# Routed attention of a four-layer kernel: the exponentials scaled by their sums on VectorE ahead of the transposes, the reciprocals' spreading matmuls removed, the attention output copied by ScalarE

## The reference, cut to what matters

```python
def _L0_ffn_ref(x, Wq, bq, Wk, bk, Wv, bv, Wr, br, Wo, bo):
    N_HEAD = 16; N_ACTIVE = 4; D_ATTN = 64
    dist = jax.nn.softmax(jnp.mean(x @ Wr + br, axis=1), axis=-1)
    _, idx = jax.lax.top_k(dist, N_ACTIVE)
    idx = jnp.sort(idx, axis=-1)
    ...
    Qs, Ks, Vs = (gather(Q), gather(K), gather(V))
    scale = 1.0 / jnp.sqrt(jnp.asarray(D_ATTN, x.dtype))
    score = jax.nn.softmax(jnp.einsum('bhqd,bhkd->bhqk', Qs, Ks) * scale, axis=-1)
    O = jnp.einsum('bhqk,bhkd->bhqd', score, Vs)
    O = O.transpose(0, 2, 1, 3).reshape(b, s, N_ACTIVE * D_ATTN)
    return O @ Wo + bo
```

## Time and profile before

| | us |
|---|---|
| time before, median of 3 runs | 599.1 (597.71 to 599.11) |
| the profiled execution, its own time | 606.65 |
| its span in the trace | 604.8 |
| PE busy | 511.8 (85%) |
| DVE busy | 381.9 (63%) |
| ACT busy | 272.9 (45%) |

### The profile page before, as it was taken

One profiled execution on the slowest core, in us unless ns is written; L12 is line 12 of the kernel. 1 busy time (PEld: TensorE's weight loads), 2 busy tenths in 40 slices (PEclk: granted clock), 3 DMA queues, 4 the chain that ended last, 5 costly groups with the idle time before them and its releaser, 6 DMA issues.

```text
span 604.8 us, 9328 instructions
## 1 busy us (share of the span) xinstructions
PE 511.8 (85%) x3141; PEld 354.3 (59%) x3141; DVE 381.9 (63%) x1362; ACT 272.9 (45%) x842; POOL 152.5 (25%) x179
## 2 busy tenths in 40 slices
PE   3921899978879899989878978979999999689976
PEld 2300788956744467675546445765666666358845
DVE  4899958462684576844659446755444444699766
ACT  2778557331223566613344425623222222489453
POOL 4999943040247000002102531110000000300032
PEclk9755599989798999997886977987999999899989
DMA  7003000000281000000010030000000000000001
GB/s 271 28 10 130 2 2 1 2 1 28 112 348 51 1 2 1 2 2 1 0 32 21 22 94 1 2 1 1 1 1 1 1 0 2 0 1 1 3 0 36
DMA packets 8197, 18.37 MB, mean 30 GB/s; under 512 B 1043, under 2 KB 6227, under 8 KB 7638
## 3 DMA queue, kind: packets, MB, share of 16 engines
q1 hardware_dynamic: 8150, 17.78, 8.2%
HBM read 15.99 MB, written 1.79 MB: 29 GB/s over the span
## 4 chain that ended last, share of the span: by engine, by line
PE 66%; POOL 13%; DVE 11%; ACT 5%; issue 3%; DMA 1%; SPq 0%; DVEq 0%; POOLq 0%; ACTq 0%
PE bank L1775 6%; PE bank L1776 6%; PE bank L1786 6%; PE bank L248 3%; PE bank L1022 3%; PE bank L1961 3%; PE bank L762 3%; PE bank L1066 3%; PE bank L1045 2%; POOL rstd L206 2%; PE bank L1937 2%; PE bank L728 2%; ACT arenaB L1977 2%; PE bank L241 2%; PE bank L843 2%
## 5 line engine op out<-in xcount | busy, mean ns | idle before, releaser
L205 POOL TENSOR_SCALAR rtmp<-mv 128x4 f32<-128x4 f32 x22 | 5.1, 231 | 329.3 <-DVE mv L191 329.2
L1827 DVE TENSOR_TENSOR arenaB<-arenaB,bank 128x512 f32<-128x512 f32 x40 | 27.5, 687 | 54.9 <-PE bank L1776 54.0
L1797 ACT ACTIVATE arenaB<-bank 128x512 f32<-128x512 f32 x40 | 24.0, 599 | 76.9 <-PE bank L1775 76.8
L1786 PEld LDWEIGHTS bank<-arenaA,arenaB 128*128 128x128 f32 x320 | 38.7, 192 | 9.1 <-issue 9.1
L248 PE MATMUL bank<-in_ctx 128*128 128x512 f32 (+1 forms) x114 | 43.4, 528 | 0.0
L1775 PE MATMUL bank<-xnT,arenaA 128*128 128x512 f32 x80 | 42.8, 618 | 0.0
L1776 PE MATMUL bank<-xnT,arenaA 128*128 128x512 f32 x80 | 42.0, 606 | 0.0
L1786 PE MATMUL bank<-arenaA,arenaB 128*128 128x128 f32 x320 | 38.8, 275 | 0.0
L248 PEld LDWEIGHTS bank<-in_ctx 128*128 128x128 f32 x114 | 20.3, 210 | 17.7 <-issue 17.5
L1977 ACT ACTIVATE arenaB<-bank,arenaB 128x77 f32<-128x77 f32 x88 | 27.2, 347 | 5.9 <-DVE arenaB L2000 5.9
L1776 PEld LDWEIGHTS bank<-xnT,arenaA 128*128 128x128 f32 x80 | 15.8, 197 | 20.2 <-issue 20.2
(11 more groups left out here) (472 smaller groups left out, 1283.3 us busy)
## 6 DMA issues: line engine op xcount, KB each, us to landing
arenaA<-in_moe_dram SPq DMA_DIRECT2D x1, 3840.0 KB, 11.5
in_dft<-in_dft_dram SPq DMA_DIRECT2D x1, 2048.0 KB, 7.5
in_dft<-in_head_dram SPq DMA_DIRECT2D x1, 2048.0 KB, 7.6
arenaA<-in_l_dram SPq DMA_DIRECT2D x1, 2048.0 KB, 16.0
vw_scratch<-in_dft SPq DMA_DIRECT2D x32, 38.5 KB
arenaB<-vw_scratch SPq DMA_DIRECT2D x2, 576.0 KB, 4.8
in_rows<-in_rows_dram SPq DMA_DIRECT2D x1, 842.5 KB, 7.2
in_ctx<-in_ctx_dram SPq DMA_DIRECT2D x1, 653.0 KB, 6.5
```

Source lines behind the costliest of these rows:

```text
L1786: ins = nc.tensor.matmul(bank[4 + m % 3][:, q4 * P:(q4 + 1) * P], hid2[:, m % 2, c, q4 * P:(q4 + 1) * P], w[:, 2 * HE + c * P:2 * HE + (c ...
L1797: nc.scalar.activation(sil2[:, n % 3, :], bank[n % 2][:], ACT.Silu).then_inc(silu_ready, 1)
L1827: Vv.tensor_tensor(hid2[:, m % 2, c, :], sil2[:, n % 3, :], bank[2 + n % 2][:], ALU.mult).then_inc(hid_ready, 1)
```

## The change

The division moves. DVE, right behind the reciprocals of unit n-1, multiplies each head's exponentials (128x512, in place in `pb0`) by their reciprocal, a pointer scalar. PE's turn of unit n-1 no longer waits for the exponentials but for these products, head by head (`p_norm`). The spreading matmuls, the copy of their result on ACT and DVE's multiplication of the output go. The output is copied from its bank to `oT0` by ACT, behind the exponentials of the pass. The other hunks only take the 16 counts of the stage off the semaphore `rb_copy` and `rb_mm` that a later stage shares.

```diff
@@ pe_attend0
                 m = n - 2
                 if 0 <= m < NU:
                     t, pair = m // 2, m % 2
-                    own, other = bank[6 + m % 2], bank[6 + (m + 1) % 2]
-                    pe.wait_ge(rinv_ready, m + 1)
-                    if m:
-                        pe.wait_ge(o_norm, m)
-                    for i in range(2):
-                        h = 2 * pair + i
-                        ins = nc.tensor.matmul(other[DF * i:DF * (i + 1), AT_R], rinv0[:, t, h:h + 1].broadcast_to([P, DF]), ident,
-                                               start=True, stop=True)
-                    ins.then_inc(rb_mm, 1)
+                    own = bank[6 + m % 2]
                     pe.wait_ge(pT_dve, m + 1)
                     pe.wait_ge(pT_act, m + 1)
-                    if m:
-                        pe.wait_ge(rb_copy, m)
+                    if m >= 2:
+                        pe.wait_ge(o_copy, m - 1)
...
                 m = n - 1
                 if 0 <= m < NU:
-                    pe.wait_ge(sc_exp, 2 * (m + 1))
...
                     for i in range(2):
+                        pe.wait_ge(p_norm, 2 * m + i + 1)
                         for k in range(TB):
@@ vec_attend0
                     Vv.reciprocal(rinv0[:, t, hs], rsum0[:, t, hs]).then_inc(rinv_ready, 1)
+                    dve.wait_ge(rinv_ready, m + 1)
+                    for i in range(2):
+                        h = 2 * (m % 2) + i
+                        Vv.tensor_scalar(pb0[:, m % 2, i, :], pb0[:, m % 2, i, :], rinv0[:, t, h:h + 1], None, ALU.mult).then_inc(p_norm, 1)
                 m = n - 2
-                if 0 <= m < NU:
-                    dve.wait_ge(rb_copy, m + 1)
-                    dve.wait_ge(pv_mm, m + 1)
-                    if m >= 4:
-                        dve.wait_ge(wo_mm, m // 2 - 1)
-                    Vv.tensor_tensor(oT0[:, m % 4, :], bank[6 + m % 2][:, AT_O], rb0[:, m % 2, :], ALU.mult).then_inc(o_norm, 1)
@@ act_attend0
             for n in range(NU + 2):
-                m = n - 2
-                if 0 <= m < NU:
-                    act.wait_ge(rb_mm, m + 1)
-                    if m >= 2:
-                        act.wait_ge(o_norm, m - 1)
-                    nc.scalar.copy(rb0[:, m % 2, :], bank[6 + (m + 1) % 2][:, AT_R]).then_inc(rb_copy, 1)
                 if n < NU:
...
+                m = n - 2
+                if 0 <= m < NU:
+                    act.wait_ge(pv_mm, m + 1)
+                    if m >= 4:
+                        act.wait_ge(wo_mm, m // 2 - 1)
+                    nc.scalar.copy(oT0[:, m % 4, :], bank[6 + m % 2][:, AT_O]).then_inc(o_copy, 1)
                 m = n - 1
                 if 0 <= m < NU:
                     act.wait_ge(sc_turned, 2 * m + 2)
```

More of the change, by code:

```diff
@@ L883, in program @@
         pT0 = part(arenaB, 10240, 2, 2, S)
-        rb0 = part(arenaB, 13056, 2, P)
         oT0 = part(arenaB, 13312, 4, P)
@@ L900, in program @@
         sc_mm, sc_max, sc_exp, sc_turned = sem("sc_mm"), sem("sc_max"), sem("sc_exp"), sem("sc_turned")
-        pT_dve, pT_act, pv_mm, o_norm, wo_mm, x_added = (
-            sem("pT_dve"), sem("pT_act"), sem("pv_mm"), sem("o_norm"), sem("wo_mm"), sem("x_added"))
+        pT_dve, pT_act, pv_mm, o_copy, p_norm, wo_mm, x_added = (
+            sem("pT_dve"), sem("pT_act"), sem("pv_mm"), sem("o_copy"), sem("p_norm"), sem("wo_mm"), sem("x_added"))
         rinv_ready, rb_mm, rb_copy = sem("rinv_ready"), sem("rb_mm"), sem("rb_copy")
@@ L1049, in pe_attend0 @@
                     t = m // 2 - 1
-                    pe.wait_ge(o_norm, m)
-                    pe.wait_ge(rb_copy, min(m + 1, NU))
+                    pe.wait_ge(o_copy, m)
                     for c in range(2):
@@ L1641, in pe_attend2 @@
                     if t:
-                        pe.wait_ge(rb_copy, NU + t)
+                        pe.wait_ge(rb_copy, t)
                     for k in range(TB + 1):
@@ L1653, in pe_attend2 @@
                     pe.wait_ge(oT2_ready, t + 1)
-                    pe.wait_ge(rb_copy, NU + min(t + 2, NT))
+                    pe.wait_ge(rb_copy, min(t + 2, NT))
                     nc.tensor.matmul(bank[6 + t % 2][:, AT_W], oT2[:, t % 2, :], V["wo2T"], start=True, stop=True).then_inc(wo2_mm, 1)
@@ L1696, in vec_attend2 @@
                 if 0 <= t < NT:
-                    dve.wait_ge(rb_copy, NU + t + 1)
+                    dve.wait_ge(rb_copy, t + 1)
                     dve.wait_ge(pv2_mm, t + 1)
@@ L1721, in act_attend2 @@
                 if 0 <= t < NT:
-                    act.wait_ge(rb_mm, NU + t + 1)
+                    act.wait_ge(rb_mm, t + 1)
                     if t >= 2:
```

## The result

The changed kernel takes 614.3 us (median of 4 runs, 612.94 to 617.19) against 599.1. The ratios of this text come from the fast runs of both kernels (a fourth run of the kernel before, at 609.23, was a slow one) and not from the two medians, whose quotient would be 1.0254; this one is 1.0214, 95% interval 1.0149 to 1.0278. The changed kernel took nearly the same time in both; the kernel before was faster in its few first runs. By the two ratios the change makes the kernel slower by 10 to 13 us; 9.9 were forecast. Both intervals are clear of no change; only the second point estimate lies under 2%, and neither interval excludes 2%.

The account below looks back on a forecast made before the run. PE was taken to bound the stage, then a loop through DVE. Terms +0.9, +7.5, +0.7 and +0.8 gave +9.9 us on 606.65, 1.63%, so 599.1 x 1.0163 = 608.9 us; range about 604.5 to 615.

Parts of the forecast that it names:

- the loop: In each pass: scores, both maxima, reciprocals, one scaling, turn, next scores; pass 4.13 us long; chance 80%.
- The signs: Changed profile: PE about 75%, turn released by DVE's scaling, about 480 ns; equal 4.13 us passes; DVE idle before maxima; clock 1.00.
- three signs of being wrong: Maxima sooner than 1.16 us after the scores, scaling under 0.3 or over 0.6 us, or clock below 1.00 before 263 us.
- The removal: Spreading matmuls taken from PE: 0.27 us a pass, a gain only if PE stays full, which was not expected.
- start: First turn of the stage, held until the first scaling is done: +0.9 us.
- middle: Units 2 to 15: 13 passes of 4.13 us, 53.7 against 46.20, +7.5 us.
- the layer norm: Inside passes 11 and 12, its DVE work delays the maxima by 0.4 and 0.3 us: +0.7 us.
- The end: Value products of unit 14 wait for ACT's copy, 4.90 instead of 4.09 us after the last scores: +0.8 us.
- The clock: Rival: PE's rests drop the granted clock to 0.50, about 30 us more, about 639 us in full; chance 5%.
- The copy on ACT: New output copy behind the exponentials is off the path; without that cover, less than 0.3 us a pass.
- The rival that ends faster: PE stays the bound because scaled exponentials are ready in time; about 596 us; chance 3%.
- The rival of one element a cycle: DVE's scaling takes 0.69 us, the pass becomes 4.44 us; about 613.5 us; chance 8%.

Follow-up runs that it names:

- e2: Changed kernel with the scaled exponentials written to an unread tile and the turn waiting for the unscaled exponentials again; ratio to the kernel before 0.9985, stage 59.14 us.
- e5: Changed kernel with one more scaling of the same size, into an unread tile, between reciprocals and first scaling; one profile, stage 77.00 us, passes 4.58 and 4.59.
- e6: Changed kernel with reciprocals and both scalings of unit n-1 moved ahead of the maxima of unit n on DVE; ratio to the kernel before 0.9982, stage 61.82 us.
- e7: Changed kernel with reciprocals and both scalings moved between the first and second maximum of a pass on DVE; one profile, stage 65.26 us.
- e3: Changed kernel without scalings or their wait, spreading still removed, DVE multiplying the output by a constant tile; ratio to the kernel before 0.9916, stage 57.72 us.
- e1: The changed kernel run again, unedited, beside the kernel before; ratio 1.0167 (1.0122 to 1.0211), medians 613.4 against 604.4 us, stage 72.67 us.
- e11: The changed kernel profiled a third time, unedited, for the clock alone; own time 608.94 us, stage 72.29 us.
- e4: Changed kernel with filler matmuls in PE's waits ahead of the turns and the last two value products; ratio to the kernel before 1.0186, stage 70.44 us.

## Why the prediction was right

**The bound and the loop.** Right in mechanism and near in size. The turn is released at 3.19 instead of 3.11 and the pass is 4.19 instead of 4.13. The scaling was well priced; the difference is the time from its end (225.90 + 0.48 = 226.38) to PE's weight load (226.50), 0.12 where 0.07 was taken from ACT's copy, and another 0.03 from the load to the first transpose, which the sum left out. e2 shows that the wait alone makes the loop, e5 that what stands in it counts one to one, e6 and e7 that DVE's order decides where the scaling stands in it.

**The signs.** Of those that the prediction named, the equal passes, the releaser, the 480 ns and DVE's idle time ahead of the maxima came out. PE was to be busy for about 75% and was for 83% (34.73 of 42 us): the 3.05 of 4.13 that it took for a pass leaves out the projection, which stands in every second one, as its own 2.6 says. And one of its three signs of being wrong appeared: the clock fell below 1.00 in the stage.

**The removal.** 0.27 in a pass was forecast if PE stayed full; e3 measured 0.22, the distance in passes rather than between starts.

**Term by term**, e1 against before: start 5.38 - 4.41 = +1.0 (0.9 forecast); middle 54.83 - 46.21 = +8.6 (7.5 and 0.7 for the layer norm, 8.2). In it the layer norm's passes are 4.46 and 4.32, 0.4 over 4.19 together and not 0.7: in the first profile of the change the maxima start 1.47 (249.95 - 248.48) and 1.30 (254.24 - 252.94) into these passes instead of 1.17, so they are late by 0.30 and 0.13, where 0.4 and 0.3 were worked out. The end: 10.84 - 10.06 = +0.8 where the clock holds (e11), as forecast. Together 10.4 against 9.9.

**The clock**, given 5% as a rival in full, came in a small part: about 1.2 us at the start (5.13 - 4.19 and 5.66 - 5.38) and 1.6 at the end (12.46 - 10.84), each in some executions. That is the step of the prediction that was too confident. It argued from 200 to 208 that a PE busy for 71% keeps its clock, and for the passes this held: 1.00 in the middle of e1. What it did not look at are the single rests ahead of and behind them. Before, PE waited 1.40 ahead of the first turn; the change made it 2.40, as a row above shows, and the sum had priced only the 0.9 of delay.

**The copy on ACT** cost nothing in the passes, as forecast: it follows the last accumulator read, and ACT then idles for 0.75 until the turn is done. The rival that ends faster did not happen; e3 shows what it would have been worth. The rival of one element a cycle is excluded by the 484 ns, and so is the 0.33 us that the prediction kept apart from its sum.

**The whole.** 10.4 us and up to 2.8 for the clock are 1.7 to 2.2% of the profiled 606.65; the two comparisons gave 1.67 and 2.14%, where 1.63 was forecast. Since the change is in the stage and the scatter is outside it, I take the difference between the two for scatter and these falls, which no run here separates.

**Where luck had a part.** The forecast in us, 608.9, hangs on the 599.1 of three runs. The measured 614.3 is 5.4 above it and only 0.7 below the upper end of the range, which was set at 615 for a slow scaling that did not come. Of the 5.4, 2.4 come from that base: 599.1 x 1.0214 is 611.9. The sound test is the ratio, and both intervals hold the 1.0163. The prediction also took 0.3% for the least difference that can be told; the intervals here reach 0.3 to 0.65% to either side.

## What to carry to other kernels

An engine at 100% tells what removing its work is worth, not what a new wait costs it: lay one pass out with its start as zero, mark when the operand of the new wait can be ready, and compare with the moment at which the waiting engine gets there. Here 0.22 us a pass was removed and the turn moved back by 0.88, since the new work stood behind two maxima in VectorE's order that had to wait for scores themselves. Before giving up such a change, try the same instructions at another place: ahead of the maxima, or with a buffer and a pass between maker and user, the same arithmetic came out within 1.5 us of the stage before (61.82, 60.49 and 59.19 against 60.68), though short of the 57.72 of the removal alone; but a longer pipeline pays at its end what it gains in the middle when it has only 16 units.

## What the hardware showed that I had not expected

- The granted clock fell to 0.50 behind a PE wait of 2.40 us in three of four profiles of the changed kernel's start (and in none of the one with 2.79 and the two with 2.21), and behind passes with rests of 0.4 and 1.04 and one of 0.72 in two of three; the pass at the start costs 5.13 us then instead of 4.19. With fillers ahead of the turns, two profiles out of two were free of it.
- A PE at rest starts 0.15 us after the end of the scaling that it waits for (226.38 to 226.53); kept busy with fillers, 0.06 us after it (225.16 to 225.22 in e4).
- Two scalings in a row take 0.88 us, 0.40 from start to start, though one is 484 ns long; the three of e5 follow each other by 0.40 too.
- Taking four matmul instructions away that start 0.27 us ahead of the next group shortened a full PE's pass by 0.22.
